# Copying transposed attention weights out of PSUM with two engines instead of one, in the first batch of an experts block

## The reference, cut to what matters

```python
def attention(x, ...):
    ...                                  # k, q with rotary halves, v
    scores = jnp.einsum('bqhd,bkhd->bhqk', q, k) * scale
    causal = jnp.tril(jnp.ones((s, s), dtype=bool))
    scores = jnp.where(causal[None, None], scores, jnp.finfo(scores.dtype).min)
    probs = jax.nn.softmax(scores, axis=-1)
    out = jnp.einsum('bhqk,bkhd->bqhd', probs, v).reshape(b, s, H)
    return out @ o_w

h = x + attention(rmsnorm(x, ln1_w), ...)
out = h + moe(rmsnorm(h, ln2_w), ...)
```

## Time and profile before

| What | Value |
|---|---|
| Median of 3 runs | 1849.79 us (1848.68 to 1850.85) |
| The profiled execution | 1844.72 us, span 1842.9 us |
| PE busy in the span | 1595.7 us (87%) |
| DVE, ACT, POOL busy | 1375.4, 1181.6 and 601.2 us (75%, 64%, 33%) |
| Attention of the first batch alone | from 1368.1 to about 1443.8 us |
| The four head groups in it, start of `look` 1 to start of `look` 1 | 17.6 us each |

### The profile page before, as it was taken

One profiled execution on the slowest core, in us unless ns is written; L12 is line 12 of the kernel. 1 busy time (PEld: TensorE's weight loads), 2 busy tenths in 40 slices (PEclk: granted clock), 3 DMA queues, 4 the chain that ended last, 5 costly groups with the idle time before them and its releaser, 6 DMA issues. The chain is left out here.

```text
span 1842.9 us, 25960 instructions
## 1 busy us (share of the span) xinstructions
PE 1595.7 (87%) x7554; PEld 1120.9 (61%) x7554; DVE 1375.4 (75%) x3613; ACT 1181.6 (64%) x2865; POOL 601.2 (33%) x1908
## 2 busy tenths in 40 slices
PE   5799999989748889978898879888879899999987
PEld 2546656565646667866786668766645556555554
DVE  6666757562359999999999999999744565776646
ACT  3244343412159999999999999999637665665630
POOL 3504233240134455545554455544310100101000
PEclk9799999999888889999998889988989999999989
DMA  5000000000300000000000000000000000000000
GB/s 227 1 1 1 1 1 1 1 1 0 109 1 1 1 1 1 1 1 1 1 1 1 1 1 1 1 1 1 1 0 1 1 1 1 1 13 1 12 1 23
DMA packets 6717, 19.23 MB, mean 10 GB/s; under 512 B 1072, under 2 KB 4144, under 8 KB 5296
## 3 DMA queue, kind: packets, MB, share of 16 engines
q1 hardware_dynamic: 6576, 17.58, 2.6%
HBM read 15.48 MB, written 2.10 MB: 10 GB/s over the span
## 5 line engine op out<-in xcount | busy, mean ns | idle before, releaser
L1610 ACT ACTIVATE mem_arena<-mem_arena,r_shift 128x256 f32<-128x256 f32 x864 | 385.2, 511 | 23.0 <-POOL r_shift L1529 23.0
L1340 DVE BATCH_NORM_STATS2 r_moments<-mem_arena 128x6 f32<-128x512 f32 x576 | 379.9, 690 | 9.4 <-ACT mem_arena L1610 6.3
L1689 PE MATMUL r_bank<-arena,r_wT 128*128 128x256 f32 x1024 | 232.3, 386 | 4.2 <-ACT mem_arena L1610 3.7
L1689 PEld LDWEIGHTS r_bank<-arena,r_wT 128*128 128x128 f32 x1024 | 195.1, 194 | 35.3 <-issue 9.0
L1705 PE MATMUL r_bank<-ident,mem_arena 128*128 128x128 f32 x576 | 109.6, 322 | 71.8 <-DVE mem_arena L1356 71.7
L1317 DVE MAX8 r_top<-r_bank 128x8 f32<-128x256 f32 x384 | 145.3, 405 | 17.1 <-PE r_bank L1689 16.9
L1699 PE MATMUL r_bank<-arena,ident 128*128 128x256 f32 x384 | 142.4, 458 | 12.6 <-ACT r_wT L1636 12.4
L2243 ACT ACTIVATE arena<-arena,e_NM 128x512 f32<-128x512 f32 (+3 forms) x256 | 134.3, 558 | 29.5 <-DVE e_NM L1931 29.5
L1705 PEld LDWEIGHTS r_bank<-ident,mem_arena 128*128 128x128 f32 x576 | 79.8, 164 | 114.1 <-DVE mem_arena L1356 104.6
L1689 PE MATMUL r_bank<-arena,r_xnT 128*128 128x256 f32 x512 | 120.8, 396 | 24.1 <-ACT mem_arena L1610 23.7
L1610 ACT ACTIVATE r_u<-r_u,r_shift 128x256 f32<-128x256 f32 x288 | 131.8, 510 | 5.6 <-POOL r_shift L1529 5.6
(11 more groups left out here) (328 smaller groups left out, 3222.1 us busy)
## 6 DMA issues: line engine op xcount, KB each, us to landing
w<-in_w SPq DMA_DIRECT2D x3, 1024.0 KB, 14.4
out_x<-X SPq DMA_DIRECT2D x4, 512.0 KB, 2.9
X<-in_x SPq DMA_DIRECT2D x1, 1536.0 KB, 10.6
w_in<-in_w_in SPq DMA_DIRECT2D x1, 1156.0 KB, 6.4
mem_arena<-in_wq SPq DMA_DIRECT2D x1, 1024.0 KB, 17.5
mem_arena<-in_wo SPq DMA_DIRECT2D x1, 1024.0 KB, 21.0
gate<-in_gate SPq DMA_DIRECT2D x1, 1024.0 KB, 7.8
up<-in_up SPq DMA_DIRECT2D x1, 1024.0 KB, 9.8
```

The costliest lines, as they stand in the source:

```text
L1340: last = dve.bn_stats(moments[:, a.lane, 2 * p:2 * p + 2, :].rearrange("p two c -> p (two c)"), u[a.lane][:, 2 * p:2 * p + 2, :].rearrange ...
L1610: last = act.activation(u[a.lane][:, h, :], u[a.lane][:, h, :] if k else scores[:, h, :], ACT.Relu, bias=shift[:, a.lane, h:h + 1])
L1689: last = pe.matmul(scores[:, h, :], lhs, (G1 if a.first else G2)[:, h, i, :], start=i == 0, stop=i == 1)
```

## The change

In the attention of the first batch (a = 0) the copies of blocks 1, 3, 5, 7 and 9 of each head group are taken off ACT's queue and put on DVE's, as a `tensor_scalar` that multiplies by 1.0. They have a semaphore of their own, `dve_copied`; `act_copied` counts what ACT has left to copy. PE's waits for free banks and for the ten copies of a head group are changed accordingly. DVE's instruction list for this attention is a function of its own, `alone`; the tests for b = -1 in DVE's `overlap` go. Everything from `middle(0)` on does the same as before. PE's list of matmuls is the same.

```diff
+    DVE_TURNS = (1, 3, 5, 7, 9)
...
+    def act_copied(a, g, n):
+
+        mine = NT - len(DVE_TURNS)
+        return g * mine + n if a == 0 else NG * mine + ((a - 1) * NG + g) * NT + n
...
     def t_turns(a, g, *rs):
         for r in rs:
-            t_take(a, g, r, "copied", (a * NG + g) * NT + r + 1)
+            if a == 0 and r in DVE_TURNS:
+                t_take(a, g, r, "dve_copied", g * len(DVE_TURNS) + DVE_TURNS.index(r) + 1)
+            else:
+                t_take(a, g, r, "copied", act_copied(a, g, r + 1 - sum(d < r for d in DVE_TURNS if a == 0)))
...
+            def keep(g, *rs):
+
+                for r in rs:
+                    i, kb = TURNS[r]
+                    dve.wait_ge(R["tr"], g * NT + r + 1)
+                    if g:
+                        dve.wait_ge(R["pv_done"], g)
+                    dve.tensor_scalar(PT[kb][:, :, (i - kb) * P:(i - kb + 1) * P],
+                                      bank[t_bank(0, g, r)].rearrange("p (j q) -> p j q", j=4), 1.0, None,
+                                      ALU.mult).then_inc(R["dve_copied"], 1)
...
+            def alone():
+
+                for g in range(NG):
+                    take(0, g, 0, 1)
+                    if g:
+                        keep(g - 1, 9)
+                    take(0, g, 2, 3)
+                    take(0, g, 4, 5)
+                    keep(g, 1)
+                    take(0, g, 6, 7)
+                    keep(g, 3)
+                    if g:
+                        divide(0, g - 1)
+                    take(0, g, 8, 9, 10, 11)
+                    keep(g, 5)
+                    keep(g, 7)
+                    if g == 0:
+                        normed_rows(0)
+                    if g == 1:
+                        row_stats(1)
+                    if g == 3:
+                        rms_rows(1)
+                keep(NG - 1, 9)
+                divide(0, NG - 1)
+
...
                     take(a, g, 0, 1)
-                    if work and g:
+                    if g:
                         combine(b, e0 - 2, 1)
                     take(a, g, 2, 3)
-                    if work:
-                        gated(b, e0)
-                        hide(b, e0)
+                    gated(b, e0)
+                    hide(b, e0)
...
-            for b in range(-1, B - 1):
+            middle(-1)
+            alone()
+            for b in range(B - 1):
                 middle(b)
                 overlap(b)
...
             def keep(a, g, *rs):
 
                 for r in rs:
+                    if a == 0 and r in DVE_TURNS:
+                        continue
                     i, kb = TURNS[r]
                     act.wait_ge(R["tr"], seq(a, g) * NT + r + 1)
...
             def weigh(a, g):
 
-                pe.wait_ge(R["copied"], (seq(a, g) + 1) * NT)
+                pe.wait_ge(R["copied"], act_copied(a, g, NT - (len(DVE_TURNS) if a == 0 else 0)))
+                if a == 0:
+                    pe.wait_ge(R["dve_copied"], (g + 1) * len(DVE_TURNS))
                 t_free(t_use[a, g, "values"])
                 o = bank[t_bank(a, g, "values")]
```

More of the change, by code:

```diff
@@ L1848, in experts_block @@
         names = ("zeros", "stats", "rms", "xr", "xT_in_psum", "xT", "lat_done", "lat", "a_done", "parts", "rot", "kq", "qt",
-                 "v_done", "v", "look", "take", "exp", "tr", "copied", "pv_done", "ot", "o_rows", "ao", "aot_in_psum", "aot",
+                 "v_done", "v", "look", "take", "exp", "tr", "copied", "dve_copied", "pv_done", "ot", "o_rows", "ao", "aot_in_psum", "aot",
                  "proj_done", "h", "ms", "r3", "hn", "hT_in_psum", "hT", "logits_done", "logits", "expl", "gate_done",
@@ L2043, in middle @@
                     route(b)
+            def alone():
[21 more added lines that the diff above has]
+                divide(0, NG - 1)
             def overlap(b):
-                a, work = b + 1, b >= 0
+                a = b + 1
                 for g in range(NG):
@@ L2064, in overlap @@
                         divide(a, g - 1)
-                    if work:
-                        gated(b, e1)
+                    gated(b, e1)
                     take(a, g, 8, 9, 10, 11)
[L2068 to L2071, removed]
+                    hide(b, e1)
+                    combine(b, e0, 0)
+                    if g == 0:
                         choose(b)
-                    if work and b and g == 2:
+                    if b and g == 2:
                         out_rows(b - 1)
@@ L2080, in overlap @@
                         rms_rows(a + 1)
-                if work:
-                    combine(b, 6, 1)
-                    combine(b, 7, 0)
+                combine(b, 6, 1)
+                combine(b, 7, 0)
                 divide(a, NG - 1)
-                if work:
-                    combine(b, 7, 1)
+                combine(b, 7, 1)
             def experts(b):
```

## The result

With the change the kernel takes 1846.83 us (median of 20 runs, 1841.03 to 1851.04), without it 1849.75 us (median of 20, 1845.35 to 1857.01). The ratio is 0.998 with a 95% interval of 0.9972 to 0.9989: about 3.7 us faster by the ratio (2.0 to 5.2 by its interval), 2.9 us by the medians. The forecast of 1846.2 us and its range held.

What follows compares the result with a forecast made beforehand. PE was taken as the bound, ACT second, DVE half empty. Terms of 1.8, 1.3, 0.85 and -0.3 us summed to 3.65, said as 3.6, off the median 1849.79: 1846.2 us, range 1843.9 to 1848.6.

Steps and rivals of the forecast that it cites:

- Term 1: PE's waits ahead of block 3 and the previous group's rows shrink as ACT's queue loses block 1's copy: 1.8 us gained.
- Term 2: PE's block 4, waiting for exponential 7 on ACT, starts earlier in all four head groups: 1.3 us gained.
- Term 3: Last group's block 8, waiting for exponential 11, starts earlier as copies 5 and 7 leave ACT: 0.85 us gained.
- Term 4: Product with the values: gains in groups 0 and 2, losses in 1 and 3 behind DVE's row work; sum -0.3 us.
- rival c: PE's half-rate clock stretches: the shift adds or removes one of about 1.5 us, giving 1847.7 or 1844.7; chance 0.18.
- The copy's price: One DVE copy from PSUM taken as 0.69 us, and 0.61 us from start to start.
- rival a: DVE's copy has another price: gain 4.75 us at 0.46 us a copy, 1.5 at 0.99; chance 0.12.
- Rival b: DVE becomes the bound if copies are dear: gain gone near 1.1 us, 4 us slower at 1.3; chance 0.07.
- Rival d: The gain is absorbed by a later stage waiting for something that did not move: 1849.8 us; chance 0.05.
- A clock under 1.00 between 1373 and 1440: Sign in the changed profile, around the first batch's attention, that the prediction would be wrong.
- the last group's product later than 1436.2: Sign that the prediction would be wrong: start of the last head group's product with the values in the changed profile.

Runs made afterwards that it cites:

- the moved row work: The change, with DVE's deferred row work moved behind the fourth maximum of a later look 0; median 1844.21 us, ratio 0.997 to the kernel before.
- row work later, no filling: The change with DVE's deferred row work moved and the first batch's clock-keeping matmuls left out; median 1840.48 us, ratio 0.9949 to the kernel before.

## Why the prediction was right

The start of each piece against the second look of group 0, before minus after, gives each term its measured size.

- **Term 1, up to the rows.** Forecast 1.8 us, measured 1.84: 0.38 in group 0 and 0.48 or 0.49 up to the rows in each of the others. The wait ahead of block 3 is gone in all of them. The experiment with blocks 1 and 3 alone shows that this and term 2 are theirs.
- **Term 2, block 4.** Forecast 1.3, measured 1.44: 0.58 in group 0 and 0.24 in each of the others, as worked out. The rest is 0.07 us from block 4 to the look behind it in groups 1 and 2 (2.88 us before, 1397.86 to 1400.74; 2.81 after, 1401.57 to 1404.38). The prediction counted the idle time only; behind a wait the piece itself is longer too (block 4 took 1.09, and takes 1.04 without a wait).
- **Term 3, block 8 of the last group.** Forecast 0.85, measured 0.91. Its idle row fell from 1.44 to 0.61.
- **Term 4, the product.** Forecast -0.3, measured about -0.07: the term that was mis-sized most. By group: 4.08, 4.54 and 3.91 us from look 0, where 4.10, 4.63 and 3.97 were worked out, and 2.11 from block 8 in the last, where 2.2 was. All four were worked out a little too long. In group 1 the step that can be seen is `row_stats`: it holds DVE for 1.77 us (1405.09 to 1406.86), not 1.84, since its last aggregate overlaps the maximum behind it, and copy 7 starts at 0.10 as said. The mechanism, row work ahead of a maximum or a copy, is what the moved row work shows: without it the product comes 3.91 us behind the look in each group. In the last group 0.19 of the 0.27 us lost went with `rms_rows`; the other 0.08 stayed and was not traced.
- **Sum.** Forecast 3.65, measured 4.14 in S, and 3.7 by the ratio of the timed runs. That the median of 1846.83 lies 0.6 us from the forecast is in part luck: the interval of the ratio is 3.2 us wide, and rival c's 1847.7 lies hardly further off. The terms are borne out by S and by the rows, not by the total.
- **The copy's price.** 0.69 us was taken from a plain copy out of PSUM, and 20 rows have 0.691 as their median. The source and not the instruction's kind set it (a `tensor_scalar` within SBUF takes 459 ns), and rival a did not happen. The estimate of 0.66 us worked out from the Trainium skill (VectorE: DVE Perf Modes, the section on the TRN2 errata) is 5% below this, so the trace doesn't bear out the extra 0.15 us.
- **Rival b, DVE as the bound.** It did not happen at 0.69, and the doubled copy shows that it is real. By the prediction's own rule (2 us for each 0.1 above 1.1) a copy of 1.46 us would be 7.2 us slower than before. S was 11.8 us longer than before, 6.3 with the clock's part taken off. What the rule lacked is the half clock: with waits of 2.04, 2.49 and 1.99 us ahead of three of the four products, these ran at half rate in whole or in part, while the one behind 1.16 us took its 2.36.
- **Rival c, the clock.** It took place in the profiled execution, in the last overlap and in layers that the change doesn't touch, and with the 5.59 us ahead of the change it is why that execution is longer than that of before: 5.59 - 4.14 + 2.1 = 3.5 us. In the touched stretch the clock is 1.00 throughout S, as expected.
- **Rival d.** Ruled out by 400.6 and 402.7 us behind the stretch, with 3.4 us more at half clock in the last overlap; with blocks 1 and 3 alone, where that half clock did not come, 400.4 us lie behind it.

Two of the signs that the prediction named were badly put, as points in time. A clock under 1.00 between 1373 and 1440 is there, from 1374.7 to 1378.1, but it is the stretch that lies from 1369.2 to 1372.6 before, ahead of S in both. The other is the last group's product later than 1436.2. It starts at 1440.66, but everything ahead of the change came 5.56 us later. Against the second look of group 0 it starts 62.33 us behind, 4.13 less than before. A sign of this kind has to be a distance within one trace. The others held: groups of 16.44, 17.06 and 16.44 us where 16.5, 17.2 and 16.6 stood, twenty copies of 0.69, and waits of the product of 1.02 in groups 1 and 3 against 0.40 in group 2.

The chances were nearly even between faster and no change that can be told, since the gain lies on the edge of what a measurement tells. It came out as 0.2%, with an interval of 0.11 to 0.28%: less time than before, and not told whether over or under 0.2%.

## What to carry to other kernels

Where one engine's queue holds both what PE waits for next and copies that PE needs only later, give some copies to the half-empty engine and put its deferred work behind the instructions that PE waits for, not ahead of them. Matmuls that only keep the clock up are fixed work of the bound engine: once the waits that they covered are short, try without them, and keep them where the clock is seen to fall. Let the distance that is compared begin ahead of everything that the edit touches. Compare distances within a trace before comparing totals, when a clock outside the change moves the totals by more than the change.

## What the hardware showed that was not expected

- The point at which the first batch's attention begins varies by as much as most edits here move the time. Its first look started between 1366.82 and 1380.21 us in twelve profiled executions of programs that are the same up to there; one and the same kernel (row work later, no filling) had it at 1372.80 and at 1380.21. It goes with the time at half clock ahead of it, 205 to 249 us. What sets whether the clock falls after a given gap in the layers ahead was not tried.
- The same product ran at half clock in some places and not in others, and the wait just ahead of it does not tell which. Behind 1.65 us it took 2.36, 2.36 and 3.92 us, behind 0.74 us 3.90 (all before, without filling), behind 2.04 us 3.93 and behind 1.16 us 2.36 (copy made twice). Behind 1.08 us, in the kernels with shared copies and without filling, it took 2.36. What else decides stays open.
- The drain between two DVE copies costs 0.16 us: they start 0.77 apart (1.46 - 0.69), where a copy and its successor without one start 0.61 apart.
